# Mixture-of-experts layer behind cross-attention: the gathered rows of an expert are transposed ahead of the gate and up product, not behind it

## What is computed

```python
scores = softmax(xf @ gate_w.T); topk_w, topk_idx = top_k(scores, 6)      # T = 2048 rows
buf_tok, buf_w = ...            # per expert up to 128 row numbers and their weights
gx = xp[buf_tok]                                        # gather: 64 x 128 x 512
gu = einsum('ech,ehi->eci', gx, gate_up_proj)           # 512 -> 2 x 192
g, u = split(gu, 2)
hid = silu(g) * u
eo = einsum('eci,eih->ech', hid, down_proj) * buf_w[..., None]   # 192 -> 512
routed = zeros.at[buf_tok].add(eo)                      # scatter-add
shared = silu(xf @ sg.T) * (xf @ su.T) @ sd.T           # one shared expert, inner size 384
out = x + routed + shared
```

## Time and profile before

| | |
|---|---|
| median of 3 runs | 783.82 us (783.07 to 786.35) |
| profiled execution | 784.43 us, its span 782.5 us |
| mean granted TensorE clock | 0.992 |
| PE busy | 752.1 us (96%) |
| DVE busy | 604.2 us (77%) |
| ACT busy | 448.8 us (57%) |
| POOL busy | 314.7 us (40%) |
| memory traffic | 238 GB/s over the span; 341 to 387 GB/s in most slices of the expert phase |

### The profile page before, as it was taken

How to read it: one execution, slowest core, us unless ns; L and a number is a source line. 1 busy time by engine, 2 the same in 40 slices (tenths; PEclk the granted TensorE clock), 3 DMA queues, 4 the chain that set the end, 5 groups by cost and what they waited for, 6 DMA issues and landing times.

```text
span 782.5 us, 10839 instructions
## 1 busy us (share of the span) xinstructions
PE 752.1 (96%) x3766; PEld 637.6 (81%) x3766; DVE 604.2 (77%) x1194; ACT 448.8 (57%) x795; POOL 314.7 (40%) x258
## 2 busy tenths in 40 slices
PE   7999999999999999999999999999999999989983
PEld 6887888878888788888888889989889888878762
DVE  6549576886678775884686899999999999989622
ACT  4424333343344234353154899998998999979610
POOL 3000010545004550066315355566657676665530
PEclk9999999999999999999999999999999999999997
DMA  5932554735666347252567999999999999999878
GB/s 177 276 69 108 172 206 173 166 118 164 255 193 167 110 165 267 70 142 88 203 259 230 374 337 351 359 354 343 352 347 349 354 343 352 342 349 344 192 173 204
DMA packets 86244, 187.68 MB, mean 240 GB/s; under 512 B 26016, under 2 KB 32544, under 8 KB 82592
## 3 DMA queue, kind: packets, MB, share of 16 engines
q1 hardware_dynamic: 54688, 141.84, 49.8%
q0 software_dynamic: 18480, 39.93, 22.0%
q10 hardware_dynamic: 13024, 5.25, 2.8%
HBM read 143.33 MB, written 42.87 MB: 238 GB/s over the span
## 4 chain that ended last, share of the span: by engine, by line
PE 77%; DMA 8%; issue 4%; ACT 3%; POOL 3%; DVE 3%; ACTq 1%; SPq 0%; POOLq 0%
PE bank L1250 10%; PE bank L1252 10%; PE bank L1251 10%; PE ps_gu L1250 4%; PE ps_gu L1252 4%; PE ps_gu L1251 4%; PE scores L1250 3%; PE scores L1252 3%; PE scores L1251 3%; PE ps_dn L1250 3%; DMA second_sum<-eo,idx_all 3%; PE ps_dn L1252 2%; PE ps_dn L1251 2%; PE ps_xgT L1782 2%; DMA second_sum<-product,idx_all 2%
## 5 line engine op out<-in xcount | busy, mean ns | idle before, releaser
L496 POOL DMA_INDIRECT table<-rows,slot x72 | 83.3, 1157 | 144.4 <-DVEq L982 110.8
L1646 DVE TENSOR_TENSOR gu_lo<-raw,gu_hi 128x768 fp32r<-128x768 f32 x126 | 120.3, 956 | 9.0 <-ACT gu_hi L1554 7.4
L1554 ACT ACTIVATE gu_hi<-raw 128x768 fp32r<-128x768 f32 x128 | 107.2, 840 | 0.0
L1250 PE MATMUL ps_gu<-gu_hi,xgT_hi 128*128 128x384 f32 x256 | 91.7, 358 | 0.0
L1252 PE MATMUL ps_gu<-gu_hi,xgT_lo 128*128 128x384 f32 x256 | 86.8, 339 | 0.0
L1251 PE MATMUL ps_gu<-gu_lo,xgT_hi 128*128 128x384 f32 x256 | 86.6, 338 | 0.0
L531 ACT ACTIVATE qT<-bank 128x512 fp32r<-128x512 f32 x32 | 19.1, 598 | 108.4 <-PE bank L1252 78.7
L1503 POOL DMA_INDIRECT xg<-x_rows,idx_all x39 | 48.0, 1230 | 45.3 <-PE ps_xgT L1782 18.9
L536 ACT ACTIVATE pbuf<-scores,negmax 128x1024 f32<-128x1024 f32 x16 | 17.8, 1114 | 64.2 <-DVE negmax L732 58.9
L674 DVE TENSOR_TENSOR qT<-bank,qT 128x512 fp32r<-128x512 f32 x32 | 22.0, 687 | 39.5 <-ACT qT L531 39.5
L1511 POOL DMA_INDIRECT out_rows<-product,idx_all x24 | 41.3, 1722 | 18.2 <-DMA out_rows<-eo,idx_all 8.8
(11 more groups left out here) (299 smaller groups left out, 2202.1 us busy)
## 6 DMA issues: line engine op xcount, KB each, us to landing
raw<-expert_in SPq DMA_DIRECT2D x64, 1024.0 KB, 11.6
rest<-rest_in SPq DMA_DIRECT2D x32, 256.0 KB, 11.9
x_rows<-pbuf SPq DMA_DIRECT2D x17, 256.0 KB, 2.1
stage<-wkT_in SPq DMA_DIRECT2D x4, 1024.0 KB, 5.3
stage<-ctxT_in SPq DMA_DIRECT2D x4, 1024.0 KB, 7.5
stage<-wvT_in SPq DMA_DIRECT2D x4, 1024.0 KB
stage<-ctx_in SPq DMA_DIRECT2D x4, 1024.0 KB, 9.6
stage<-woT_in SPq DMA_DIRECT2D x4, 1024.0 KB
```

What stands on the lines that cost most here:

```text
L496: pool.indirect_dma_start(out=table, out_offset=bass.IndirectOffsetOnAxis(ap=slot[:, i, k:k + 1], axis=0), in_=rows[:, i, k, :], in_offset ...
L1250: pe.matmul(out, still[0], moving[0], start=first, stop=False)
L1554: act.activation(gu[n % GU_SLOTS][0][part], gate_up_of(n, part), ACT.Copy).then_inc(weights_high, 1)
L1646: return dve.tensor_tensor(lo, x, hi.bitcast(F32), ALU.subtract)
```

## The change

In each expert step the three engines take `rows(e + 4)`, `high_xgT(e + 4)` and `low_xgT(e + 4)` further to the front. On PE the four transposes stand behind `transpose_hidden(e + 1)` and ahead of `gate_up(e + 2)`. On ACT and DVE the operand of the expert e + 4 is made right behind the silu and the product `up`, ahead of the second half of the weights of e + 3.

```diff
 # ACT
             if e + 2 < E:
                 gate(e + 2)
+            if e + 4 < E:
+                high_xgT(act, e + 4)
             if e + 3 < E:
                 act_weights(act, PIECE_NO["gu", e + 3, 1], PIECE_NO["gu", e + 3, 1] + 1)
-            if e + 4 < E:
-                high_xgT(act, e + 4)
 # DVE
             if e + 2 < E:
                 up(dve, e + 2)
+            if e + 4 < E:
+                low_xgT(dve, e + 4)
             if e + 3 < E:
                 dve_weights(dve, PIECE_NO["gu", e + 3, 1], PIECE_NO["gu", e + 3, 1] + 1)
-            if e + 4 < E:
-                low_xgT(dve, e + 4)
 # PE
             if e + 1 < E:
                 transpose_hidden(e + 1)
+            if e + 4 < E:
+                rows(pe, e + 4)
             if e + 2 < E:
                 gate_up(pe, e + 2)
-            if e + 4 < E:
-                rows(pe, e + 4)
```

## The result

The changed kernel takes 789.34 us (median of 8 runs, 787.69 to 791.86), the kernel before 785.32 (8 runs, 783.07 to 786.37). The ratio is 1.0058, 95% interval 1.0044 to 1.0071: slower by 0.6%, 4.5 us by the ratio and 4.0 by the medians, just beyond the bound of 0.5%. The prediction started from a median of 783.82 us over 3 runs of the kernel before; over 8 runs it is 1.5 us higher. The profiled execution took 788.74 us against 784.43, with a span of 786.9 us against 782.5.

A forecast was written before the change was run, and what follows sets the result against it. PE and DVE share the bound, the chain of adds is third. Stalls of 9.0 us less ACT's 2.56 make experts 6.4 late, costing +1.3: 784.43 + 1.3 = 785.7, less 0.6 to the median, 785.1 us; range 781 to 791.

The forecast's parts named there:

- rival 1: Whole kernel: PE's wait comes through, adds follow engines or stalls exceed their spare time; 791.3 us, chance 0.25.
- The new wait: PE in short steps: moved transposes wait for DVE's low part of the gathered rows, a stall of 0.5 us each.
- How often: PE up to step 53: one stall in each of 18 groups, 18 x 0.5 = 9.0 us.
- the stated upper end: PE's stalls: at most 0.6 us for all 26 short steps of the groups, 15.6 us.
- The last ten steps: From step 54 on: the new loop takes 4.44 us, just under DVE's 4.49, so nothing is added.
- ACT and DVE: Second half of gu_lo ends 0.6 us later, hidden by the later product; 0.2 a step if that cover failed.
- The adds: POOL's chain: rows near 651 come 7.0 us later with 7.1 to spare, so adds go on within 0.3.
- The adds' early start: POOL near 510: the add can go about 2.3 us earlier, but later rows eat the gain.
- The end: After the experts, 6.4 us late: adds cost 0 to 2.5 us, middle +1.3; read back within 2 us of 755.3.
- two level paths: At the end: adds and PE's tail, whose last sum starts at 772.7 against 772.31; the later, the adds, counts.
- The gathers: Last gathers: moved transposes would wait 1.1 us for their rows, but not with everything 6.4 later.
- The page's price: POOL's adds: 2.6 us each by the skill page; adds would never be behind and the time would be 792.

The follow-up runs named there:

- e1: Kernel before with only PE's transposes moved ahead of the gate and up product, ACT and DVE as before: 821.45 us, ratio 1.0465.
- e6: Changed kernel with small adds, each carrying 16 of 128 rows: 786.86 us, ratio 1.0024 to the kernel before.
- e5: Kernel before with small adds, each carrying 16 of 128 rows: 772.17 us, ratio 0.983.
- e2: Kernel before with only ACT and DVE in the new order, PE as before: 785.29 us, ratio 1.0005.
- e11: Kernel before with the new order on all three engines for e < 42 only: 788.96 us, ratio 1.0059.
- e12: Kernel before with the new order on all three engines for e >= 42 only: 786.40 us, ratio 1.0015.
- e3: Changed kernel, but PE's transposes go early only in steps that follow a step with shared work: 789.46 us, ratio 1.0059 to the kernel before.
- e8: Changed kernel, but PE's transposes go early only in ten steps between two shared halves: 787.54 us, ratio 1.0027 to the kernel before.
- e9: Kernel before with POOL's adds ahead of its gathers for the first 18 experts: 785.35 us, ratio 1.0007.
- e4: Changed kernel with a third high buffer, gathered rows' operands made ahead of silu and up: 785.44 us, ratio 1.0009 to the kernel before.
- e10: e8 plus POOL's adds ahead of its gathers for the first 18 experts: 787.36 us, ratio 1.0021 to the kernel before.
- e7: Kernel before with POOL's adds ahead of its gathers for the first 14 experts: 785.34 us, ratio 1.0002.

## Why the prediction held, and where not

The forecast of 785.1 us was 4.2 below the median, of which 1.5 are the low median over 3 runs that it started from; the change itself was forecast at +1.3 us and measured at +4.0. The time lies in the range of 781 to 791, between the forecast and rival 1, and the likeliest verdict, the same within 0.5%, was missed by a little: the ratio of 1.0058 is slower.

- *The new wait.* Right in mechanism, and in size for one: 1.59 us from silu to transposes on paper, 1.69 in the trace, a loss of 0.45 to 0.5 per short step. Three steps take 15.0 us (transposes at 497.82 and 512.82), as stated. e1 confirms it.
- *How often.* This step failed. "In the second of them PE already waits for DVE and uses up that slack, so I count one stall of 0.5 each": groups with a shared down product lose 0.9, both short steps in full. The engines lose 11.7 us by step 51, not 9.0; the stated upper end, all 26 short steps, was the right count (24 of them by step 51). PE's later product also makes ACT and DVE later, and DVE's waits for dn_hi are 24 instead of 3. That this is where the slack went is argued, not shown.
- *The last ten steps.* Worked out as free (4.44 against 4.49 us). With small adds, where nothing else disturbs, the lag of e6 over e5 goes from 11.7 at step 51 to 14.1 at step 63: 0.2 a step.
- *ACT and DVE.* "Hidden" is right in the changed kernel (one wait of 0.3 us). Where the cover is gone it costs what e2 shows, 0.3 us a group.
- *The adds.* The chain of adds was rightly named a bound of its own (e5), and as the path that sets the end. But it was forecast 1.3 us late, and it is 4.45 late at the read back. Because of the count, the rows near 651 came 9.2 us late instead of 7.0, which is past the spare time of 7.1 and past the threshold of 0.51 us a group that rival 1 names (0.66 measured). The add there left 2.9 late instead of on time. In the last ten steps, where rows are late again (732.75), the last add became 4.3 late. That the place near 651 decides is only in part shown: e11, new up to there, has the whole loss, and e12, new behind it, little or none; but e3's adds are late long before it, and e8's only at the very end. How much of the engines' delay an add takes over therefore stays open.
- *The adds' early start.* "The gain is eaten" holds: -0.1 to +1.5 us near 505 to 515 in the trace. e9 makes it likely that it would not have come without a stall either.
- *The end.* ACT's wait of 2.56 us went, as predicted; the experts end 11.0 us late, not 6.4. The read back is 4.45 late, not within 2. PE's pause is gone, but the low clock isn't, and the last sum starts 6.4 us late instead of 0.4. The prediction took the end as the later of two level paths. The traces show one: some 27 us behind the start of the read back, whatever PE's tail does. It was right that the adds count, and 3.2 us short in how late they are.
- *The gathers* bound nothing, as forecast for late engines.
- *The page's price.* The Trainium skill (DMA: Bandwidth & Descriptors, Anatomy of one DMA — SWDGE (gpsimd) path) gives an estimate of 2.6 us for an add. The links in the changed kernel keep to 8.8 to 9.0 us under load, and the last adds land 4.7 to 5.4 us after issue. The measurement decides: the adds hide most of the engines' loss, and the time is not the 792 that this price would give.

## What to carry to other kernels

Moving an instruction that waits ahead of a long product puts everything behind it under its wait: work out the chain from the product before to that wait, compare it with the work in the whole gap between the two products, and count every gap that is shorter, also those where the engine already seems to have slack. If a second chain (here the adds) runs behind the engines, a delay of the engines can be paid from its spare time: 5 or 6 us cost nothing in e2 and e4, 11 us cost 4. Don't read the cost off the smallest spare time alone, as e3 and e8 show, but follow the second chain to the step that sets the end. Small copies of the hidden traffic, as in e5 and e6, show what a change costs the engines when its time shows little.

## What the runs showed of the hardware

The same pause of PE was followed by either of the two levels of the clock. All 14 traces have a pause of 2.22 or 2.23 us ahead of the first tail product. In the kernel before, e1, e2, e3, e11 and e12 the matmuls behind it kept to 0.23 us each (granted clock 1.00, 2.4 GHz; in the kernel before in 755 to 760 us). In the changed kernel and in e4 to e10 they went over to 0.43 us each, 1.2 GHz, soon after it; in the changed kernel the granted clock was 0.69 in 770 to 775 us. Nor did the longer pause decide: 4.34 us in the kernel before was followed by 0.66, 3.04 us in e11 by 1.00. In none of the traces with full adds did it move the end, since that hangs on the read back.

Behind the adds, the read back, the merges and the last stores took the same time in every kernel with full adds: 26.9 to 27.3 us, with the DMA engines 93 to 104% busy from 757 to 780 us in the kernel before and 98 to 108% from 761 to 784 in the changed one.

A link of the chain of adds nearly kept its length while weights were being loaded, with engines up to 12 us late: over stretches of eight links 8.7 to 8.8 us in the kernel before, 8.8 to 9.0 in the changed one, 8.5 to 9.3 over e3 and e7 to e12. In e1, with engines up to 37 us late and adds waiting for rows, it was 8.5 to 10.2. That is, traffic that is spread over 11 us more did not make an add land sooner. The memory traffic in these slices of the kernel before is 337 to 374 GB/s (its table says 341 to 387).
